# A spike-coded two-layer FFN: first layer over gathered w1 rows in two groups instead of over all 512 channels

## The chip, the core and the metric

The kernel runs on one core of one Trainium2 chip. The metric is the device time of one execution in microseconds; the kernel before takes 104.52 us in the median of 3 runs (104.49 to 104.67). The profile was taken in a further execution of 103.89 us, whose instructions span 102.1 us. Engines: PE (matrix unit; its weight load is PEld), DVE (vector), ACT (scalar), POOL (GpSimd), and SP, which only issues transfers. Two batches (b = 0, 1) of 2048 tokens with 512 channels; all data is float32.

## What is computed

```python
rates  = relu(x) * 0.001
c      = cond[:, None, :] + cumsum(rates, axis=1)      # per batch and channel
spikes = (floor(c) - floor(c one token before)) / 0.001
h      = relu(spikes @ w1 + b1)                        # 512 -> 2048
out    = x + h @ w2 + b2                               # 2048 -> 512
```

A channel climbs by less than one over a batch in nearly all cases, so it spikes at most once (with these inputs never more). Most of the 4096 tokens have no spike: their row is x plus one fixed row (the "idle row", relu(b1) @ w2 + b2). Counted from the reference's inputs: 421 and 427 channels spike in the two batches, on 386 and 380 different tokens; 33 and 40 of these tokens have more than one spiking channel, with 35 and 47 channels beside the first one of their token.

## The kernel before

The work has four parts, and their order on each engine is written out by hand.

**Table.** For a token with exactly one spiking channel the FFN's result depends on the channel alone. A table of 512 such rows (less the idle row) is computed for every channel: ACT turns each of the 16 chunks of transposed w1 into `relu(1000 * w1 + b1) - relu(b1)` (`table_chunk`, L419), and PE multiplies them with w2 into four PSUM banks (`table_part`, L799): 64 matmuls of 512 columns.

**Where the spikes are.** DVE sums relu(x) over each block of 16 tokens (`block_totals`), PE makes running sums (`sum_totals`), DVE finds the block in which each channel crosses its level (`find_blocks`), POOL fetches the 16 values of that block for each channel from a transposed copy of x (4 indirect transfers per batch, L342), and DVE finds the token (`find_bases`, `find_tokens`). PE copies the tokens along a row (`spread_tokens`), and DVE compares each channel's token with all others' (`count_met`): a channel alone on its token is a "single", the first one of several is a "lead" (`find_leads`). Leads get a slot number (`count_leads`, `find_slots`).

**Crowded tokens.** PE finds the token of every slot (PE's `find_slots`), DVE builds a 0/1 matrix of 512 channels by 128 slots (`first_spikes`, `second_spikes`), and `first_layer` (L883) multiplies w1 with it: 16 chunks of 4 matmuls, with 2 PSUM banks in turn, each emptied by ACT (L452). `second_layer` (L892) is 16 matmuls of 512 columns. DVE adds x and b2 (L729), and POOL writes the rows to their places (L381).

**All other rows.** The idle row is `idle_by_hand` on DVE for the first 9 chunks (`BY_HAND`), and `add_strips` and `join_strips` on PE for the rest. `add_idle` adds it to all of x in SBUF: DVE by four token rows at a time (L673), POOL by one (L354), in quarters (b, q). SP stores the eight quarters of 1 MB each in the fixed order (0,0), (0,3), (0,1), (0,2), (1,3), (1,0), (1,1), (1,2) (L303), each after a wait for its adds. Then POOL adds the table rows onto the rows of singles with indirect accumulating transfers, 4 per batch (L347). Those of batch b wait for `idle_stored[b]`, that is until all four stores of that batch have landed, and the first also for `singles_listed` and for `table_rows_ready`, ACT's copies of the table out of PSUM (L458), which stand between the first layer's evictions. The last write of new rows is behind them in POOL's order. POOL may touch x rows only between marks (`reading_psum`) that DVE sets.

The program ends when the last scatters and the write at L381 have landed. SP's queue also loads w1 (4 MB in 4 transfers, L297) behind all other loads.

## Time and profile before

| | |
|---|---|
| median of 3 runs | 104.52 us (104.49 to 104.67) |
| the profiled execution | 103.89 us, span 102.1 us |
| PE busy | 95.4 us (93%) |
| DVE busy | 65.9 us (64%) |
| POOL busy | 43.2 us (42%) |
| ACT busy | 35.5 us (35%) |
| moved by DMA | 31.66 MB, mean 310 GB/s |
| granted TensorE clock | 0.99 of full speed |

The span is cut into stages: table and search for spikes until about 68 us, first layer until 83 us, second layer until 97 us, and a tail of 4.7 us. Beside the two layers, SP stores the eight quarters (from 56 to 87 us) and POOL issues the scatters (from 77 to 95 us). Busy shares are averages over these stages; what one stage is worth shows in the waits and in the chain of work that ended last.

### The profile page before, as it was taken

How to read it: one execution, taken by the hardware profiler on the slowest of the kernel's cores; microseconds unless marked ns; L12 is line 12 of the kernel's file. 1: busy time of each engine (PE TensorE's matmuls, PEld its weight loads, DVE VectorE, ACT ScalarE, POOL GpSimd, SP SyncE). 2: the span in 40 equal slices, each digit the busy share in tenths (PEclk: the TensorE clock that was granted, in tenths of full speed). 3: DMA queues.
4: the chain of work that ended last, by engine and by line, in shares of the span. 5: the costliest groups of instructions: out<-in, count | busy, mean ns of one | idle time of the engine just before them, and what ended most of it. 6: DMA issues, size and time to landing. Idle time of an engine off the chain costs nothing.

```text
span 102.1 us, 1157 instructions
## 1 busy us (share of the span) xinstructions
PE 95.4 (93%) x370; PEld 54.0 (53%) x370; DVE 65.9 (64%) x142; ACT 35.5 (35%) x64; POOL 43.2 (42%) x44
## 2 busy tenths in 40 slices
PE   5999999999999999999969999999999999999910
PEld 5944444444644444644234564649999984444300
DVE  2448999888699999488958888899993020020020
ACT  2796515315372540569740000003953330000000
POOL 6350000000078700017508181499937883688040
PEclk9999999999999999999999999999999999999996
DMA  1999999999999999999999725427999999998701
GB/s 58 286 387 414 417 420 411 411 407 409 409 409 409 396 393 401 409 394 387 379 373 352 324 116 218 193 125 292 395 430 436 407 336 195 218 115 106 92 8 62
DMA packets 10028, 31.66 MB, mean 310 GB/s; under 512 B 1671, under 2 KB 1799, under 8 KB 8994
## 3 DMA queue, kind: packets, MB, share of 16 engines
q1 hardware_dynamic: 8304, 29.63, 74.7%
q0 software_dynamic: 1568, 1.90, 11.4%
q8 instruction: 5, 0.08, 0.3%
q14 instruction: 5, 0.04, 0.1%
q10 hardware_dynamic: 146, 0.01, 0.1%
HBM read 21.58 MB, written 10.75 MB: 316 GB/s over the span
## 4 chain that ended last, share of the span: by engine, by line
PE 50%; DVE 20%; POOL 13%; issue 11%; ACT 1%; POOLq 1%; DVEq 0%
PE ps_table L807 40%; DVE x_sb L673 11%; POOL out L347 11%; PE ps_small L900 4%; DVE same L600 3%; PE ps_idle L823 2%; PE ps_turn L844 2%; DVE hot L619 1%; PE ps_idle L827 1%; PE ps_idle L833 1%; DVE spk_t L634 1%; POOL out L381 1%; POOL general_x L370 1%; POOLq L258 1%; DVE spk_t L629 1%
## 5 line engine op out<-in xcount | busy, mean ns | idle before, releaser
L807 PE MATMUL ps_table<-w_sb 128*128 128x512 f32 x128 | 56.9, 595 | 0.0
L807 PEld LDWEIGHTS ps_table<-w_sb 128*128 128x128 f32 x128 | 23.6, 190 | 27.1 <-issue 26.4
L342 POOL DMA_INDIRECT rates<-in_x_turned,sixteen_at x8 | 9.9, 1236 | 33.9 <-DVE sixteen_at L563 32.1
L354 POOL TENSOR_TENSOR x_sb<-x_sb,idle_row 128x512 f32<-128x512 f32 x12 | 14.9, 1277 | 9.9 <-DVEq L706 3.7
L422 ACT ACTIVATE w_sb<-w_sb,b_col 128x512 f32<-128x512 f32 (+2 forms) x19 | 12.2, 643 | 16.5 <-DMA w_sb<-in_w_pairs 16.3
L549 DVE SCALAR_TENSOR_TENSOR total_two<-x_sb,total_two 128x1024 f32<-128x1024 f32 x14 | 17.1, 1225 | 1.2 <-DMA x_sb<-in_x 0.8
L347 POOL DMA_INDIRECT out<-w_sb,to_single x8 | 12.5, 1558 | 5.8 <-issue 3.7
L895 PE MATMUL ps_table<-w_sb 128*128 128x512 f32 x32 | 14.0, 595 | 0.0
L423 ACT ACTIVATE w_sb<-w_sb,minus_relu_b 128x512 f32<-128x512 f32 (+2 forms) x19 | 12.3, 649 | 0.6
L673 DVE TENSOR_TENSOR x_sb<-x_sb,ps_idle 128x2048 f32<-128x2048 f32 x5 | 11.2, 2283 | 1.5 <-ACT idle_row L448 1.3
L895 PEld LDWEIGHTS ps_table<-w_sb 128*128 128x128 f32 x32 | 6.0, 190 | 7.2 <-issue 6.9
L452 ACT ACTIVATE w_sb<-ps_turn,b_col 128x128 f32<-128x128 f32 x8 | 2.9, 367 | 19.0 <-PE ps_turn L888 18.4
L888 PE MATMUL ps_small<-spk_t,w_sb 128*128 128x128 f32 x64 | 8.5, 275 | 0.0
L888 PE MATMUL ps_turn<-spk_t,w_sb 128*128 128x128 f32 x64 | 8.5, 275 | 0.0
L888 PEld LDWEIGHTS ps_turn<-spk_t,w_sb 128*128 128x128 f32 x64 | 7.9, 192 | 0.5 <-DVE spk_t L634 0.3
L888 PEld LDWEIGHTS ps_small<-spk_t,w_sb 128*128 128x128 f32 x64 | 7.8, 192 | 0.0
L509 DVE SCALAR_TENSOR_TENSOR idle_part<-w_sb,relu_b,idle_part 128x512 f32<-128x512 f32 x9 | 6.7, 750 | 1.5 <-DMA w_sb<-in_w_pairs 1.4
L729 DVE TENSOR_TENSOR w_sb<-ps_table,general_x 128x512 f32<-128x512 f32 x1 | 0.7, 692 | 6.3 <-PE ps_table L895 6.3
L900 PE MATMUL ps_small<-ones 128*128 128x128 f32 x16 | 3.7, 427 | 1.1 <-POOLq L320 1.1
L727 DVE TENSOR_TENSOR general_x<-general_x,b_row 128x512 f32<-128x512 f32 x1 | 0.7, 691 | 6.2 <-DMA general_x<-in_x,from_general 6.2
L900 PEld LDWEIGHTS ps_small<-ones 128*128 128x128 f32 x16 | 3.5, 330 | 1.1 <-POOLq L320 1.1
L665 DVE TENSOR_SCALAR crowd<-ps_table 128x1 f32<-128x1 f32 x1 | 0.2, 159 | 6.1 <-PE ps_table L871 6.1
(113 smaller groups left out, 65.5 us busy)
## 6 DMA issues: line engine op xcount, KB each, us to landing
x_sb<-in_x SPq DMA_DIRECT2D x16, 512.0 KB, 14.3
out<-x_sb SPq DMA_DIRECT2D x8, 1024.0 KB, 4.1
w_sb<-in_w_pairs SPq DMA_DIRECT2D x15, 512.0 KB, 15.7
w_sb<-in_w SPq DMA_DIRECT2D x4, 1024.0 KB, 15.3
w_sb<-in_w_pairs SPq DMA_DIRECT2D x2, 256.0 KB, 2.9
b_row<-in_b SPq DMA_DIRECT2D x1, 256.0 KB, 15.3
rates<-in_x_turned,sixteen_at POOLq DMA_INDIRECT x8, 6.5
out<-w_sb,to_single POOLq DMA_INDIRECT x8
```

The source lines that it names most:

```text
L342: pool.indirect_dma_start(out=rates[:, col, :], out_offset=None, in_=x_sixteen, in_offset=bass.IndirectOffsetOnAxis(ap=sixteen_at[:, col:c ...
L347: pool.indirect_dma_start(out=out_rows, out_offset=bass.IndirectOffsetOnAxis(ap=to, axis=0), in_=row, in_offset=None, bounds_check=last_ro ...
L354: last = pool.tensor_tensor(x_sb[b][:, t, :], x_sb[b][:, t, :], idle_row[:, :], ALU.add)
L422: chain(act.activation(weights, weights, ACT.Relu, bias=b1_col[:, m:m + 1], scale=PER_DT))
L423: act.activation(weights, weights, ACT.Identity, bias=minus_relu_b1[:, m:m + 1]).then_inc(table_hidden_ready, 1)
L509: step = dve.scalar_tensor_tensor(out=idle_part[:, :], in0=w2_sb[:, m, :], scalar=relu_b1[:, m:m + 1], in1=idle_part[:, :], op0=ALU.mult, ...
L549: chain(dve.scalar_tensor_tensor(out=total_two[b][:, :, :], in0=tokens, scalar=0.0, in1=total_two[b][:, :, :], op0=ALU.max, op1=ALU.add))
L673: last = dve.tensor_tensor(tokens, tokens, along(ps_idle[:, :], end - begin), ALU.add)
L807: last = pe.matmul(ps_table[c][:, :], table_hidden[:, m, c * P:(c + 1) * P], w2_sb[:, m, :], start=(m == 0), stop=(m == FC - 1))
L888: last = pe.matmul(ps_hidden[m % 2][:, 0:P], w1_sb[:, c, m * P:(m + 1) * P], spk_t[:, c, :], start=(c == 0), stop=(c == DC - 1))
L895: last = pe.matmul(ps_out[:, :], hidden[m], w2_sb[:, m, :], start=(m == 0), stop=(m == FC - 1))
L900: pe.matmul(ps_small[:, 0:P], ones[:, :], ones[:, :], start=True, stop=True)
```

## The change

First layer: POOL gathers rows of w1 (8 KB each), one for every channel that shares its token with others, into two SBUF arrays that are cleared at the start. Group 0 holds the lead channel of every crowded token, at the token's slot; group 1 holds all other channels on crowded tokens, in slots of their own. Each chunk of the first layer is then two matmuls: group 0's rows times the identity, and group 1's rows times `others_turn`, a 0/1 matrix that says to which slot's token each of the others belongs. There are three PSUM banks in turn in place of two. The 4 MB load of w1 goes away (it remains in the repeat path that these inputs don't take). To list the rows, DVE makes one-hot matrices for both groups, PE multiplies them with a small array `named` (block, token in block, row of 128, partition), and DVE turns the result into row numbers.

Around it: five chunks of the idle row by hand in place of nine, so 12 strips on PE in place of 8; another order of DVE's and PE's steps; ACT copies the table out of PSUM only after all evictions of the first layer; DVE adds the idle row to 24 token rows and POOL to 8, in place of 20 and 12.

```diff
-    BY_HAND = 9
+    BY_HAND = 5
+    GROUPS = 2
@@ SP
-            for i in range(WQ):
-                part = slice(i * (F // WQ), (i + 1) * (F // WQ))
-                sp.dma_start(w1_sb[:, :, part], w1.rearrange("(c p) f -> p c f", p=P)[:, :, part]).then_inc(w1_in[i], 16)
@@ POOL
+            for g in range(GROUPS):
+                pool.memset(spiking_rows[g][:, :], 0.0).then_inc(rows_cleared, 1)
...
+            def get_rows(b):
+                pool.wait_ge(rows_cleared, GROUPS)
+                for g in range(GROUPS):
+                    n = b * GROUPS + g
+                    pool.wait_ge(rows_listed, n + 1)
+                    if b > 0:
+                        pool.wait_ge(rows_got[g], 16 * b)
+                    pool.indirect_dma_start(out=spiking_rows[g][:, :], out_offset=None, in_=w1,
+                                            in_offset=bass.IndirectOffsetOnAxis(ap=row_at[:, n:n + 1], axis=0),
+                                            bounds_check=last_channel, oob_is_err=False).then_inc(rows_got[g], 16)
+
+            get_rows(0)
             pool.wait_ge(idle_copied, 1)
             pool.wait_ge(reading_psum, 1)
-            add_idle(0, 12, 14)
+            add_idle(0, 12, 13)
+            get_rows(1)
             pool.wait_ge(reading_psum, 2)
-            add_idle(0, 14, 16)
-            pool.wait_ge(reading_psum, 3)
+            add_idle(0, 13, 16)
             add_idle(1, 12, 16)
-            add_idle(1, 8, 12)
             pool.wait_ge(singles_listed, 1)
@@ ACT
             for m in range(FC):
                 relu_hidden(m, hidden_summed, m + 1, hidden_ready)
-                if 1 <= m <= DC:
-                    act.activation(table_row[m - 1], ps_table[m - 1][:, :], ACT.Copy).then_inc(table_rows_ready, 1)
+            for c in range(DC):
+                act.activation(table_row[c], ps_table[c][:, :], ACT.Copy).then_inc(table_rows_ready, 1)
@@ DVE, new steps
+            def list_rows(b):
+                for g in range(GROUPS):
+                    n = b * GROUPS + g
+                    dve.wait_ge(lists_found, n + 1)
+                    chain(dve.tensor_scalar(row_of[:, b, g, :], ps_list[g][:, b, 2:3], float(P), NO_ROW, ALU.mult, ALU.add))
+                    dve.tensor_tensor(row_at[:, n:n + 1], row_of[:, b, g, :], ps_list[g][:, b, 3:4], ALU.add).then_inc(
+                        rows_listed, 1)
...
+            def turn_others():
+                dve.wait_ge(row_tokens_spread, 1)
+                chain(dve.tensor_scalar(others_turn[:, :], ps_tokens, row_token[:, 1, :], None, ALU.is_equal))
+                dve.sem_inc(others_ready, 1)
@@ PE
+            def first_layer():
+                pe.wait_ge(rows_got[0], 16 * B)
+                pe.wait_ge(rows_got[1], 16 * B)
+                pe.wait_ge(others_ready, 1)
                 for m in range(FC):
-                    if m >= 2:
-                        pe.wait_ge(ready, base + m - 1)
-                    for c in range(DC):
-                        last = pe.matmul(ps_hidden[m % 2][:, 0:P], w1_sb[:, c, m * P:(m + 1) * P],
-                                         spk_t[:, c, :], start=(c == 0), stop=(c == DC - 1))
-                    yield last
+                    if m >= HB:
+                        pe.wait_ge(hidden_ready, m - HB + 1)
+                    chunk = slice(m * P, (m + 1) * P)
+                    pe.matmul(ps_hidden[m % HB][:, 0:P], spiking_rows[0][:, chunk], ident[:, :], start=True, stop=False)
+                    pe.matmul(ps_hidden[m % HB][:, 0:P], spiking_rows[1][:, chunk], others_turn[:, :],
+                              start=False, stop=True).then_inc(hidden_summed, 1)
```

**DVE, the end of the pass over x.** In the rows, `total_two<-x_sb` is one eighth of a batch in `block_totals`, `rates` to `token` is `find_tokens`, and `same,met` is `count_met`. Before, from `find_bases(0)` on:

```order
L575 SCALAR_TENSOR_TENSOR token_base<-blocks_under,far 128x4
L549 SCALAR_TENSOR_TENSOR total_two<-x_sb,total_two 128x1024
L509 SCALAR_TENSOR_TENSOR idle_part<-w_sb,relu_b,idle_part 128x512
L549 SCALAR_TENSOR_TENSOR total_two<-x_sb,total_two 128x1024 x2
L552 TENSOR_TENSOR total<-total_two 128x512
L559 TENSOR_TENSOR under<-ps_turn,theta_sum 128x512
L562 TENSOR_REDUCE blocks_under<-under 128x4
L563 SCALAR_TENSOR_TENSOR sixteen_at<-blocks_under,sixteen_f 128x4
L582 TENSOR_SCALAR rates<-rates 128x64
```

The same place in the changed kernel:

```order
L617 SCALAR_TENSOR_TENSOR token_base<-blocks_under,far 128x4
L590 SCALAR_TENSOR_TENSOR total_two<-x_sb,total_two 128x1024 x2
L624 TENSOR_SCALAR rates<-rates 128x64
L625 SCALAR_TENSOR_TENSOR climb<-token_keep,rates 128x64
L627 TENSOR_TENSOR climb<-climb,sum_at 128x64
L628 TENSOR_TENSOR under<-climb,theta 128x64
L629 TENSOR_REDUCE tokens_under<-under 128x4
L630 TENSOR_SCALAR named<-tokens_under 128x4
L631 SCALAR_TENSOR_TENSOR token<-tokens_under,token_base 128x4
L590 SCALAR_TENSOR_TENSOR total_two<-x_sb,total_two 128x1024 x2
L593 TENSOR_TENSOR total<-total_two 128x512
L644 SCALAR_TENSOR_TENSOR same,met<-ps_met,token,weigh 128x512
```

`find_tokens(0)`, which waits for POOL's four gathers of batch 0, now stands ahead of the last quarter of batch 1's sums.

**POOL, from the gathers of `rates` to the scatters.** `x_sb<-x_sb,idle_row` is one token row of `add_idle`. Before:

```order
L342 DMA rates<-in_x_turned,sixteen_at 128x16 x3
L354 TENSOR_TENSOR x_sb<-x_sb,idle_row 128x512 [waits reading_psum,idle_copied]
L354 TENSOR_TENSOR x_sb<-x_sb,idle_row 128x512
L354 TENSOR_TENSOR x_sb<-x_sb,idle_row 128x512 [waits reading_psum]
L354 TENSOR_TENSOR x_sb<-x_sb,idle_row 128x512
L354 TENSOR_TENSOR x_sb<-x_sb,idle_row 128x512 [waits reading_psum]
L354 TENSOR_TENSOR x_sb<-x_sb,idle_row 128x512 x7
L347 DMA out<-w_sb,to_single 4096x512 [waits table_rows_ready,idle_stored0,singles_listed]
```

Now:

```order
L362 DMA rates<-in_x_turned,sixteen_at 128x16 x3
L386 DMA spiking_rows<-in_w,row_at 128x2048 [waits rows_listed,rows_cleared]
L386 DMA spiking_rows<-in_w,row_at 128x2048 [waits rows_listed]
L374 TENSOR_TENSOR x_sb<-x_sb,idle_row 128x512 [waits reading_psum,idle_copied]
L386 DMA spiking_rows<-in_w,row_at 128x2048 [waits rows_got0,rows_listed,rows_cleared]
L386 DMA spiking_rows<-in_w,row_at 128x2048 [waits rows_got1,rows_listed]
L374 TENSOR_TENSOR x_sb<-x_sb,idle_row 128x512 [waits reading_psum]
L374 TENSOR_TENSOR x_sb<-x_sb,idle_row 128x512 x6
L367 DMA out<-w_sb,to_single 4096x512 [waits table_rows_ready,idle_stored0,singles_listed]
```

One token row of quarter (0,3) is added ahead of the gathers of w1's rows for batch 1, the other three behind them and behind DVE's second mark.

## Rows read from the trace of the kernel before

**Rows 1.** The page: the chain that ended last, by engine.

```profile
PE 50%; DVE 20%; POOL 13%; issue 11%; ACT 1%; POOLq 1%; DVEq 0%
```

**Rows 2.** Groups by line: count, busy us, mean ns, idle before.

```profile
L888 PE MATMUL ps_small<-spk_t,w_sb 128*128 128x128 f32 x64 | 8.5, 275 | 0.0
...
L452 ACT ACTIVATE w_sb<-ps_turn,b_col 128x128 f32<-128x128 f32 x8 | 2.9, 367 | 19.0 <-PE ps_turn L888 18.4 <-issue 0.5
```

**Rows 3.** Timeline, PE, both layers: start, duration, what.

```profile
68.93 1.05 PE L888 MATMUL ps_turn<-spk_t,w_sb 128*128 128x128 f32 x8
...
83.36 13.98 PE L895 MATMUL ps_table<-w_sb 128*128 128x512 f32 x32
```

**Rows 4.** Timeline, DVE, end of the pass over x.

```profile
36.62 1.23 DVE L549 SCALAR_TENSOR_TENSOR total_two<-x_sb,total_two 128x1024 f32<-128x1024 f32 x1
...
40.00 1.23 DVE L549 SCALAR_TENSOR_TENSOR total_two<-x_sb,total_two 128x1024 f32<-128x1024 f32 x1 [0.24 <-DMA x_sb<-in_x]
41.26 0.69 DVE L552 TENSOR_TENSOR total<-total_two 128x512 f32<-128x512 f32 x1
43.59 0.69 DVE L559 TENSOR_TENSOR under<-ps_turn,theta_sum 128x512 f32<-128x512 f32 x1 [1.63 <-PE ps_turn L844]
```

**Rows 5.** Timeline, POOL, gathers of rates.

```profile
34.53 0.96 POOL L342 DMA_INDIRECT rates<-in_x_turned,sixteen_at  x1 [0.30 <-issue]
45.58 0.94 POOL L342 DMA_INDIRECT rates<-in_x_turned,sixteen_at  x1 [10.09 <-DVE sixteen_at L563]
```

**Rows 6.** Line L342, issues at 32.5 and 34.5: issue to landing.

```profile
DMA to landing us min/median/max: 5.3/5.8/6.3
```

**Rows 7.** Groups by line, DVE and POOL.

```profile
L600 DVE SCALAR_TENSOR_TENSOR same<-ps_turn,token,weigh 128x512 bf16<-128x512 f32 x4 | 3.0, 751 | 0.4 <-PE ps_turn L856 0.3
L354 POOL TENSOR_TENSOR x_sb<-x_sb,idle_row 128x512 f32<-128x512 f32 x12 | 14.9, 1277 | 9.9 <-DVEq L706 3.7 <-DVEq L714 3.4 <-DVEq L597 2.7
L673 DVE TENSOR_TENSOR x_sb<-x_sb,ps_idle 128x2048 f32<-128x2048 f32 x5 | 11.2, 2283 | 1.5 <-ACT idle_row L448 1.3 <-DVE hot L619 0.2
```

**Rows 8.** Timeline, DVE, from find_tokens(1) on.

```profile
56.10 0.42 DVE L582 TENSOR_SCALAR rates<-rates 128x64 f32<-128x64 f32 x1
...
65.15 2.29 DVE L673 TENSOR_TENSOR x_sb<-x_sb,ps_idle 128x2048 f32<-128x2048 f32 x1 [0.24 <-DVE hot L619]
...
68.39 6.67 DVE L673 TENSOR_TENSOR x_sb<-x_sb,ps_idle 128x2048 f32<-128x2048 f32 x3
```

**Rows 9.** Line L301: the first store's landing; the fourth store's issue.

```profile
DMA to landing us min/median/max: 4.1/4.1/4.1
...
L301 SPq DMA_DIRECT2D out<-x_sb x1: 332/332/332, 70.7 to 70.7; - x1
```

**Rows 10.** Stages, busy us per engine, then clock, DMA share, GB/s.

```profile
76.00:80.00 4.00, 4.00 (x39) 4.00 (x38) 1.27 (x11) 1.63 (x5) 2.72 (x2) 1.00 0.99 410
```

**Rows 11.** DMA of 86 to 87 us: packets, MB, share of 16 engines.

```profile
q0 software_dynamic: 142, 0.19, 109.8%
q1 hardware_dynamic: 2, 0.01, 2.2%
```

**Rows 12.** Timeline, POOL, the tail.

```profile
76.98 1.61 POOL L347 DMA_INDIRECT out<-w_sb,to_single  x1 [1.92 <-issue]
...
84.45 1.01 POOL L370 DMA_INDIRECT general_x<-in_x,from_general  x1 [0.30 <-issue]
87.52 1.56 POOL L347 DMA_INDIRECT out<-w_sb,to_single  x1 [2.06 <-DMA out<-x_sb]
...
93.09 1.55 POOL L347 DMA_INDIRECT out<-w_sb,to_single  x1 [0.30 <-issue]
98.42 1.03 POOL L381 DMA_INDIRECT out<-w_sb,to_general  x1 [3.79 <-DVE w_sb L729]
```

**Rows 13.** Timeline, DVE, the new rows; line L381, issue to landing.

```profile
97.45 0.69 DVE L729 TENSOR_TENSOR w_sb<-ps_table,general_x 128x512 f32<-128x512 f32 x1 [6.32 <-PE ps_table L895]
...
DMA to landing us min/median/max: 2.7/2.7/2.7
```

More of the change, by code:

```diff
@@ L612, in find_leads @@
                 dve.sem_inc(leads_ready, 1)
             def find_slots(b):
-                mine = own(b)
                 dve.wait_ge(leads_before, b + 1)
-                chain(dve.scalar_tensor_tensor(out=slot[:, mine], in0=leads_run[:, mine], scalar=ps_small[:, b:b + 1],
-                                               in1=leads[:, mine], op0=ALU.add, op1=ALU.mult))
-                chain(dve.tensor_tensor(hot[:, mine, :], over(slot[:, mine], P), along(slot_name[:, :], DC), ALU.is_equal))
-                dve.sem_inc(hot_ready, 1)
+                for g in range(GROUPS):
+                    dve.scalar_tensor_tensor(out=slot[:, b, g, :], in0=leads_run[:, b, g, :],
+                                             scalar=ps_count[:, b, g:g + 1], in1=leads[:, b, g, :],
+                                             op0=ALU.add, op1=ALU.mult).then_inc(dve_step, 1)
@@ new lines, in find_slots @@
+                steps[0] += GROUPS
+                dve.wait_ge(dve_step, steps[0])
+                for g in range(GROUPS):
+                    dve.tensor_tensor(hot[:, b, g, :, :], over(slot[:, b, g, :], P), along(slot_name[:, :], DC),
+                                      ALU.is_equal).then_inc(hot_ready, 1)
+            def list_rows(b):
+                for g in range(GROUPS):
+                    n = b * GROUPS + g
[3 more added lines that the diff above has]
+                        rows_listed, 1)
@@ new lines, in find_row_tokens @@
+            def find_row_tokens():
+                for g in range(GROUPS):
+                    dve.tensor_copy(token_parts[:, g, :], ps_list[g][:, 0, 0:2]).then_inc(dve_step, 1)
+                steps[0] += GROUPS
+                dve.wait_ge(dve_step, steps[0])
+                for g in range(GROUPS):
+                    dve.tensor_tensor(token_parts[:, g, :], token_parts[:, g, :], ps_list[g][:, 1, 0:2],
+                                      ALU.add).then_inc(dve_step, 1)
+                steps[0] += GROUPS
+                dve.wait_ge(dve_step, steps[0])
+                chain(dve.scalar_tensor_tensor(out=row_token[:, :, :], in0=token_parts[:, :, 0:1], scalar=float(BLK),
+                                               in1=token_parts[:, :, 1:2], op0=ALU.mult, op1=ALU.add))
+                dve.sem_inc(row_tokens_ready, 1)
@@ L870, in sum_checks @@
                 pe.wait_ge(table_rows_ready, DC)
-                pe.matmul(ps_checks[:, 0:2], ones[:, :], checks[:, :], start=True, stop=True).then_inc(checks_summed, 1)
-            def find_slots(b):
-                pe.wait_ge(hot_ready, b + 1)
-                if b == 0:
-                    pe.wait_ge(met_counted, 1)
-                for c in range(DC):
-                    col = b * DC + c
-                    last = pe.matmul(ps_slots[:, b * P:(b + 1) * P], token[:, col:col + 1].to_broadcast([P, P]),
-                                     hot[:, col, :], start=(c == 0), stop=(c == DC - 1))
-                last.then_inc(slots_found, 1)
@@ L883, in first_layer, with list_rows @@
-            def first_layer(ready, base):
-                for m in range(FC):
-                    if m >= 2:
-                        pe.wait_ge(ready, base + m - 1)
+                pe.matmul(ps_checks, ones[:, :], checks[:, :], start=True, stop=True).then_inc(checks_summed, 1)
+            def list_rows(b):
+                for g in range(GROUPS):
+                    pe.wait_ge(hot_ready, b * GROUPS + g + 1)
+                    for c in range(DC):
+                        last = pe.matmul(ps_list[g][:, b, :], hot[:, b, g, c, :], named[:, b, c, :],
+                                         start=(c == 0), stop=(c == DC - 1))
+                    last.then_inc(lists_found, 1)
@@ L892, in second_layer @@
-            def second_layer(ready, base):
+                    last.then_inc(again_hidden_summed, 1)
+            def second_layer(to, ready, base):
                 for m in range(FC):
-                    pe.wait_ge(ready, base + m + 1)
-                    last = pe.matmul(ps_out[:, :], hidden[m], w2_sb[:, m, :], start=(m == 0), stop=(m == FC - 1))
+                    if m == FC // 2 and to is ps_out:
+                        sum_checks()
+                    pe.wait_ge(ready, base + (max(m + 1, OUT_FREE) if to is ps_out else m + 1))
+                    last = pe.matmul(to[:, :], hidden[m], w2_sb[:, m, :], start=(m == 0), stop=(m == FC - 1))
```

226 lines of the change are left out of this document (122 added, 104 removed).

## Prediction

> **What bounds the kernel now.** I read the chain of work that ended last, then the groups by line, then the timelines of PE, DVE and POOL, then the transfers. The chain gives PE half of the span, DVE a fifth, POOL an eighth [rows 1]. PE runs almost without a gap: the table, then from 68.93 us the first layer, and from 83.36 the second [rows 3]. DVE adds the new rows at 97.45, POOL writes them from 98.42 [rows 12, 13], and the span ends at 102.1, 3.7 us after that. So PE's two layers set the end.
>
> But a second chain ends almost as late, on DVE, the store queue and POOL: DVE's last add of the idle row ends at 75.06 (68.39 + 6.67) [rows 8]; the first scatter starts at 76.98; those of batch 1 wait for batch 1's stores until 87.52; the last one ends at 94.64 [rows 12]. It has 98.42 - 94.64 = 3.8 us of slack. That slack is what the change must not use up.
>
> **PE's part.** The first layer takes 83.2 - 68.9 = 14.3 us for 64 float32 matmuls, 0.223 each (the group rows count two passes per matmul, in two banks of 64 passes each) [rows 2, 3]. It becomes 32: 7.15 us, a gain of 7.15. ACT's evictions don't hold it: 0.37 us per chunk [rows 2] in a chunk of 0.45, and a third bank gives two chunks of time for the way round.
>
> The first layer starts later, though. PE loses eight slot matmuls (1.8 us) and gains four strips (0.9), 16 bf16 matmuls of four columns (about 1.2, an estimate between 0.5 and 1.8, since no such form is in the trace) and a transpose (0.3). It also waits in its own order for DVE, as worked out next. I find its table finished near 72.5.
>
> **DVE's part.** `find_tokens(0)` moves ahead of the last quarter of batch 1's sums. It needs POOL's fourth gather of batch 0, issued at 34.53 [rows 5] and landed 5.3 us later [rows 6], at 39.8. DVE would be there at about 37: so far `find_bases(0)` is done at 36.6 [rows 4]; the change takes one eighth of x (1.23) and two hand chunks (0.75 each) from ahead of it, and puts two eighths behind it: 36.6 - 2.7 + 2.5 = 36.4, and up to 37.5 where DVE waits for x. The gathers may be issued up to a microsecond earlier with less DVE work beside them. I take 39.2. Queued behind this wait are find_tokens (1.55 us), two eighths of x (2 x 1.26) and `total` (0.7): batch 1's total is ready at 44.0, against 41.95 [rows 4], 2.0 us late; between 0.8 (gathers a microsecond faster) and 2.7. The removed hand chunks (4 x 0.75 = 3.0 us) so buy nothing: they only lengthen the wait. PE's `sum_totals(1)` and all behind it in PE's order wait for the same.
>
> From there: 1.65 us to `under` (43.59 - 41.95, [rows 4]), 2.0 more to POOL's first gather of batch 1 (45.58 - 43.59) [rows 4, 5], three steps of 1.25 to the fourth (51.3), and 2.7 to 5.3 us to landing. The queue is empty by then, since w1 is no longer loaded; I take 3.5: 54.8. DVE's own work up to there (three compares of 0.75 [rows 7], leads, bases, slots with two one-hot writes of about 0.7, and a short wait for PE's count) comes to 54.9, so neither waits long.
>
> Then `find_tokens(1)` to the mark behind which the large adds run. Before, this took 65.15 - 56.10 = 9.05 us [rows 8]. Now: tokens 1.6; wait for PE's lists and two row lists 1.4; wait for the spread and four compares 3.8; leads 0.8; half an add 1.2; slots and two one-hots with the wait for PE 2.2; half an add 1.2; two row lists 0.85; row tokens 0.8; odd checks 1.0; `turn_others` 0.4: 15.2 us. Mark 2 comes at 70.1. Behind it DVE has five adds of 2.28 [rows 7], until 81.6, then the singles' list, 82.2.
>
> POOL in the meantime gathers w1's rows for batch 1 from 67.9 to 70.2, and only then, behind mark 2, adds the last three token rows of quarter (0,3): 3 x 1.28 [rows 7], until 73.9. The store of (0,3) is second in SP's fixed order. So only one quarter is stored before 74.2, and seven go out behind it. Before, two were gone by 66 us, and the fourth was issued at 70.7 [rows 9].
>
> **The stores.** The queue moves about 0.405 MB per us when it is full [rows 10]: 7 x 1.049 MB take 18.1 us, to 92.3. Landing adds 1.7 (4.1 for a store of 2.4 us of data) [rows 9]. The scatters of batch 0 and the fetch of x rows run beside the end. Before, five stores issued from 70.7 had landed at 87.5, 16.8 us, against 12.9 + 1.7: they lost about 2 us. I take 1.7 and get 95.7; bounds are 94.0 (nothing lost) and 99 (all of the scatters' data first).
>
> The Trainium skill ("DMA: Bandwidth & Descriptors", Queues, rings and completion order) says that each DMA engine takes turns between its queues, packet by packet. By that rule alone the scatters' five or so microseconds of engine time (an estimate) would nearly all be added to the stores, and the sum would be 3 us higher. The trace does not bear that out fully: only from 86 us, when the stores' queue is down to 2.2%, does the software queue fill the engines [rows 11].
>
> **The end.** Batch 1's scatters take 94.64 - 87.52 = 7.1 us [rows 12]: 95.7 to 102.8. POOL then loads the repeat count, which before lay in its wait: 0.3 to 1.1 us, I take 0.5. The write starts at 103.3 and the span ends 3.7 later [rows 12, 13], at 107.0, against 102.1: 4.9 us longer. The profiled execution's own time was 103.89, so 108.8; the median of the runs is 0.63 higher, so 109.4.
>
> PE's chain is done well before: its two layers end 21.4 us after the first matmul (97.45 - 68.93 - 7.15). From 73.2 that is 94.6. Its gain is covered by POOL's wait, and even a first layer that stayed at 14.3 us would end the span at about 106.5.
>
> **Rivals.**
> *PE's chain still sets the end (faster).* The place is POOL's wait for batch 1's stores. Were they landed by about 87.5, and the first scatter out by 77, POOL would be done by 94.6 and the end would be 94.6 + 4.7 = 99.3: 2.8 us less, 101.7 in the median. It decides as soon as batch 1's stores land by 87 and the table copies and the list of singles are there by 78. For it speaks PE's share of the chain [rows 1], and 4 MB less to load. Against it: the table copies now follow all evictions (73.2 + 7.15 + about 1.2 = 81.6), and seven stores from 74 can't be done by 87 at 0.405 MB per us. How late PE starts hangs on the last gather of w1's rows, issued at 69.2. The nearest rows have a landing at 2.7 us [rows 13] and one at 6.3 [rows 6]: 72 to 75.5.
> The Trainium skill (same page, "Anatomy of one DMA — SWDGE (gpsimd) path") gives about 2.0 us plus bytes over 436 GB/s; for 47 rows of 8 KB that is an estimate of 2.9 us. No row here has a gather of that size.
>
> *POOL's own work sets the end, not the stores (slower by less).* First scatter at 82.9 (singles' list 82.2), then as before 7.5 to the fetch of x, 1.3, 7.1 for batch 1 [rows 12]: 98.8, write at 99.3, span 103.0: 105.4 in the median. It needs stores landed by 91.7, so the mark and POOL's adds some 4 us earlier than I find.
>
> *DVE doesn't stall at the gather, and everything on DVE is 2 us earlier.* Same mechanism, stores land near 93.7: 107.4. It lies in the forecast's own range.
>
> *The change doesn't do what it says:* a channel list over 128 slots would start the repeat path, far slower. With 73 leads and 82 others it doesn't.
>
> **Numbers.** Forecast (stores late, scatters behind them): 0.67, its own range 106.3 to 111.5, from the bounds 94.0 and 99 of the stores and 0.8 to 2.7 of the stall. POOL's own work: 0.15. PE's chain: 0.11. Ends that cancel to about nothing: 0.03. Above 111.5: 0.04. A difference under 0.2% can't be told from none; from the same cases: faster 0.12, same 0.03, slower 0.85. Range 103.8 to 111.5: it takes in POOL's own work and leaves out the fast case.
>
> **What would show it.** Right: a wait of DVE for the gathers between the fifth and seventh eighth of batch 1, 1 us or more; `total(1)` near 44; DVE's last add near 81.6; the second store issued near 74; POOL idle before the first scatter of batch 1 with a store as what ended it, near 95.7; the first layer at 7 to 7.5 us; the chain of waits running through stores and scatters. Wrong: the write of new rows released by DVE as before; stores landed by 90; or a fill of the queue by w1's row gathers that holds PE past 78.

## The result, and the profile after

| | before | after |
|---|---|---|
| median of 4 runs on one chip | 104.5 us (103.96 to 104.67) | 109.34 us (108.88 to 109.98) |
| the profiled execution, its span | 103.89, 102.1 us | 109.98, 108.1 us |
| granted TensorE clock, mean | 0.99 | 0.94 |

The changed kernel takes 1.048 times as long (95% interval 1.041 to 1.054). The forecast was 109.4 us. Part of that closeness is luck: the forecast span was 107.0, and the spans of the four runs are 107.1 to 108.1, the profiled one being the longest; I had added 0.63 us from the profiled time to the median, and this time the median lies 0.64 below. So the mechanism is to be judged by the rows, not by the last digit.

The chain of work that ended last, by engine (answers to [rows 1]):

```profile
PE 46%; POOL 14%; DVE 13%; DMA 11%; issue 8%; POOLq 3%; ACT 1%; DVEq 0%
```

PE still has the largest share, because the chain runs back through the table. Its end is what changed. POOL's timeline (start, duration, what, in brackets the idle time before it and what ended it), which answers to [rows 12]:

```profile
68.10 0.99 POOL L386 DMA_INDIRECT spiking_rows<-in_w,row_at  x1 [5.64 <-DVE row_at L679]
69.40 1.00 POOL L386 DMA_INDIRECT spiking_rows<-in_w,row_at  x1 [0.30 <-issue]
70.43 8.65 POOL L374 TENSOR_TENSOR x_sb<-x_sb,idle_row 128x512 f32<-128x512 f32 x7
87.60 1.60 POOL L367 DMA_INDIRECT out<-w_sb,to_single  x1 [8.52 <-ACT w_sb L493]
...
95.05 1.01 POOL L402 DMA_INDIRECT general_x<-in_x,from_general  x1 [0.30 <-issue]
96.37 1.56 POOL L367 DMA_INDIRECT out<-w_sb,to_single  x1 [0.30 <-issue]
...
101.94 1.54 POOL L367 DMA_INDIRECT out<-w_sb,to_single  x1 [0.30 <-issue]
103.78 1.03 POOL L413 DMA_INDIRECT out<-w_sb,to_general  x1 [0.31 <-issue]
```

The write of new rows starts at 103.8 in place of 98.4, and follows at once on POOL's own scatters. From the first scatter on POOL works without a gap for 103.78 - 87.60 = 16.2 us. Batch 1's scatters, which I had waiting for a store, wait for nothing. The one wait is ahead of the first scatter, 8.5 us, for ACT's copies of the table (L493). The chain of waits has that place in the order of time (start, duration, engine and tile):

```profile
85.61 0.24 PE ps_turn L956 x2
85.85 0.02 issue
85.87 0.37 ACT w_sb L487
86.24 0.98 ACT w_sb L493 x2
87.22 0.37 issue
87.60 1.60 POOL out L367
```

The last chunk of the first layer, its eviction, the copies, the scatter: PE is back on the path that sets the end, though not through its second layer.

The new rows themselves are ready long before the write. DVE's timeline, as [rows 13]:

```profile
99.23 0.69 DVE L788 TENSOR_TENSOR general_x<-general_x,b_row 128x512 f32<-128x512 f32 x1 [5.45 <-DMA general_x<-in_x,from_general]
99.96 0.69 DVE L790 TENSOR_TENSOR w_sb<-ps_met,general_x 128x512 f32<-128x512 f32 x1
```

They are there at 100.65 (99.96 + 0.69), 3.1 us ahead of the write: PE's gain is covered, as forecast. PE's timeline at the first layer, answering to [rows 3], and the stages there (PE, PEld, DVE, ACT, POOL busy with counts, granted clock, DMA share, GB/s):

```profile
75.77 0.76 PE L955 MATMUL ps_turn<-ident,spiking_rows 128*128 128x128 f32 x2 [3.72 <-issue]
76.33 0.63 PE L956 MATMUL ps_turn<-others_turn,spiking_rows 128*128 128x128 f32 x2
...
82.10 0.39 PE L955 MATMUL ps_small<-ident,spiking_rows 128*128 128x128 f32 x2
```

```profile
68.00:72.00 4.00, 3.79 (x10) 1.50 (x9) 3.34 (x8) 0.00 (x0) 3.56 (x4) 1.00 0.88 297
72.00:76.00 4.00, 0.28 (x2) 0.26 (x2) 4.00 (x3) 0.00 (x0) 4.00 (x4) 0.82 0.62 248
76.00:80.00 4.00, 4.00 (x20) 4.00 (x21) 4.00 (x3) 1.47 (x4) 3.08 (x3) 0.50 1.00 412
80.00:84.00 4.00, 4.00 (x32) 4.00 (x31) 1.69 (x7) 2.56 (x7) 0.00 (x0) 0.82 1.03 426
```

PE is idle from 72.0 to 75.8, until the rows of w1 are there. Behind that wait the granted clock is 0.50, the lower of the two levels (1.2 GHz), until about 81 us: a float32 matmul (two passes in the trace, the `x2` of the rows) starts every 0.43 us there, and every 0.22 us later. The first layer takes 9.9 us (75.77 to 85.67) where I had 7.15.

### The profile page after: what moved, and what is told of

The parts are those of the page before. It is cut to its first block, busy times and chain, and to the rows that moved or that the text cites. A ratio compares the mean times of both kernels' runs of the same rounds, so it can differ in the third digit from the quotient of the medians.

```text
span 108.1 us, 1064 instructions
## 1 busy us (share of the span) xinstructions
PE 92.8 (86%) x315; PEld 48.1 (44%) x315; DVE 69.3 (64%) x163; ACT 35.4 (33%) x64; POOL 44.3 (41%) x46
## 4 chain that ended last, share of the span: by engine, by line
PE 46%; POOL 14%; DVE 13%; DMA 11%; issue 8%; POOLq 3%; ACT 1%; DVEq 0%
PE ps_table L868 27%; POOL out L367 9%; DMA rates<-in_x_turned,sixteen_at 6%; DMA spiking_rows<-in_w,row_at 5%; PE ps_small L978 3%; POOL rates L362 3%; DVE same L644 3%; DVE total_two L590 2%; DVE x_sb L736 2%; POOLq L59 2%; PE ps_turn L955 2%; PE ps_turn L905 2%; PE ps_idle L884 2%; PE ps_turn L956 2%; PE ps_small L956 1%
## 5 line engine op out<-in xcount | busy, mean ns | idle before, releaser
L868 PE MATMUL ps_table<-w_sb 128*128 128x512 f32 x128 | 58.5, 603 | 0.0
L868 PEld LDWEIGHTS ps_table<-w_sb 128*128 128x128 f32 x128 | 23.8, 193 | 27.1 <-issue 25.3
L973 PE MATMUL ps_met<-w_sb 128*128 128x512 f32 x32 | 14.1, 595 | 0.0
L736 DVE TENSOR_TENSOR x_sb<-x_sb,ps_idle 128x2048 f32<-128x2048 f32 (+1 forms) x7 | 13.5, 1979 | 0.4 <-DVE others_turn L699 0.2
L374 POOL TENSOR_TENSOR x_sb<-x_sb,idle_row 128x512 f32<-128x512 f32 x8 | 9.9, 1267 | 0.0
L973 PEld LDWEIGHTS ps_met<-w_sb 128*128 128x128 f32 x32 | 5.9, 190 | 6.7 <-issue 6.7
L386 POOL DMA_INDIRECT spiking_rows<-in_w,row_at x4 | 4.0, 1002 | 11.8 <-DVE row_at L679 11.2
L955 PE MATMUL ps_turn<-ident,spiking_rows 128*128 128x128 f32 x12 | 3.1, 354 | 3.7 <-issue 3.7
L546 DVE SCALAR_TENSOR_TENSOR idle_part<-w_sb,relu_b,idle_part 128x512 f32<-128x512 f32 x5 | 3.9, 778 | 1.6 <-DMA w_sb<-in_w_pairs 1.5
L955 PEld LDWEIGHTS ps_turn<-ident,spiking_rows 128*128 128x128 f32 x12 | 2.5, 259 | 4.5 <-issue 4.5
```

The source lines that it names most:

```text
L374: last = pool.tensor_tensor(x_sb[b][:, t, :], x_sb[b][:, t, :], idle_row[:, :], ALU.add)
L736: last = dve.tensor_tensor(tokens, tokens, along(ps_idle[:, :], end - begin), ALU.add)
L868: last = pe.matmul(ps_table[c][:, :], table_hidden[:, m, c * P:(c + 1) * P], w2_sb[:, m, :], start=(m == 0), stop=(m == FC - 1))
L955: pe.matmul(ps_hidden[m % HB][:, 0:P], spiking_rows[0][:, chunk], ident[:, :], start=True, stop=False)
L973: last = pe.matmul(to[:, :], hidden[m], w2_sb[:, m, :], start=(m == 0), stop=(m == FC - 1))
```

## The experiments

Each kernel is the changed one with the edit shown, unless said otherwise. Ratios are to the kernel before, run in turn with it on the same chip: 103.11 us for the first four, 104.18 for the next four, 104.29 for the last four. Compare ratios, best within one of these groups; the changed kernel's own are 1.048, and 1.043 when run again. A span, and every time read from a timeline, is that of one profiled execution (108.1 and 107.8 for the changed kernel); the runs of one kernel differ by about 1 us, and the profiled one can be the fastest or the slowest of them. Times of the changed kernel are from its first profile unless said otherwise.

### One wait at a time: the table copies, the clock, the second gather

**Copies early** (`e1`):

```diff
                 relu_hidden(m, hidden_summed, m + 1, hidden_ready)
-            for c in range(DC):
-                act.activation(table_row[c], ps_table[c][:, :], ACT.Copy).then_inc(table_rows_ready, 1)
+                if 1 <= m <= DC:
+                    act.activation(table_row[m - 1], ps_table[m - 1][:, :], ACT.Copy).then_inc(table_rows_ready, 1)
```

> The changed kernel, with ACT's four copies of the table out of PSUM back between the first layer's evictions of chunks 1 to 4, as in the kernel before. If the late copies hold the first scatter (87.60 in the changed kernel's trace), it now comes at 81.6 to 82.5, released by DVE's list of singles or the stores of batch 0. What ends the kernel then tells the next limit. Stores next (the prediction's mechanism): batch 1's scatters wait for a store until about 94.5, the write of new rows is at about 102, the time is about 2 us less, 107.4. PE next: no wait for stores, the write follows DVE's new rows at 100.7, 3 us less, 106.2. If the copies don't hold anything: 109.3 again.

Measured: ratio 1.063 (1.055 to 1.072), span 107.6. **PE busy** (`e2`) fills PE's wait:

```diff
             table_part(15, 1, DC)
+            for _ in range(16):
+                pe.matmul(ps_turn[:, 0:P], ones[:, :], ones[:, :], start=True, stop=True)
             first_layer()
```

> The changed kernel, with 16 matmuls of 128x128 on constants (3.6 us at full clock) between the table and the first layer, where PE now waits 3.7 us for the gathered rows; their results are overwritten. If the halved granted clock of 76 to 81 us comes from that wait, the clock stays at 1.0 there, the first layer takes 7.15 us in place of 9.9, the first scatter comes 2.7 us earlier (84.9), and the time falls by 2.0 to 2.7, to 106.6 to 107.3 (the lower saving if batch 1's stores, landed at about 94, take over). If the clock falls for another reason: 9.9 us again and 109.3. If the added matmuls delay the first layer: slower.

Measured: 1.060 (1.048 to 1.072), span 108.4. **Both** (`e3`):

> Both edits: early copies of the table and PE kept busy while it waits. First scatter at 81.6 to 82.5, DVE's new rows at about 97.9. If batch 1's stores are the next limit, batch 1's scatters start at about 94.5 as in the kernel with early copies alone, so this one is no faster than that one: 107.3. If PE is: the write at 98.2 to 99, and the time 5 us less than the changed kernel's, 104.3, even with the kernel before.

Measured: 1.065 (1.057 to 1.072), span 107.2. The changed kernel wasn't in that group of runs, so a difference of a per cent from its 1.048 can't be read out of these ratios; but they exclude that the end came forward by the 2.1, 2.8 and 4.7 us by which the first scatter did (85.54, 84.84 and 82.92). Of the 4.7 us in `e3`, 1.1 are no effect of the edits: its profiled execution is the fastest of its five, and DVE's large adds start at 68.84 there against 69.91. Where the rest went is in POOL's timeline of `e3`:

```profile
82.92 1.60 POOL L367 DMA_INDIRECT out<-w_sb,to_single  x1 [4.87 <-issue]
...
95.26 1.56 POOL L367 DMA_INDIRECT out<-w_sb,to_single  x1 [3.87 <-DMA out<-x_sb]
...
102.68 1.03 POOL L413 DMA_INDIRECT out<-w_sb,to_general  x1 [0.31 <-issue]
```

The first scatter is 4.7 us earlier, and batch 1's only 1.1, which is the 1.1 of the earlier start and nothing more, because now a store holds them. `e1` and `e2` show the same, at 95.53 and 95.90. The last store in `e3` was issued at 81.0 and took 14.0 us to land (the line of the stores, issue to landing):

```profile
DMA to landing us min/median/max: 3.9/6.9/14.0
```

So batch 1's stores land at 95.0 here (81.0 + 14.0). In the changed kernel they land sooner, though they were issued later: by 94 in its first profile, whose store queue shows no packet after that, and at 94.9 in its second (the last one issued at 82.4, 12.5 us to landing). POOL's own work is ready for batch 1 at 96.37 and 96.07, at least 2.4 us later in the one and 1.2 in the other. So an earlier first scatter goes with later stores. The rows give a reason, though no run tests it alone: the scatters' packets then run beside the last stores, and from 89 to 93 us `e3` moves 1.12 MB of stores, 0.28 MB per us (queue: packets, MB, share of 16 engines; q1 are the stores, q0 is POOL's queue):

```profile
q1 hardware_dynamic: 153, 1.12, 81.7%
q0 software_dynamic: 133, 0.17, 24.8%
```

From 86 to 87 us, with no scatter's packet beside them, the stores moved 0.43 MB in one microsecond.

The copies were at 76.0 to 78.8 in `e3` and the list of singles at 80.4, so the first scatter at 82.9 waited for a third thing, batch 0's stores, which landed at 82.1; the profile names these in `e4` and `e10`. It is the same in `e1` (landed 84.7, scatter 85.54), so its expected 81.6 to 82.5 was missed.

In `e2` the clock stays at 1.00 and the first layer takes 7.2 us (75.69 to 82.91):

```profile
76.00:80.00 4.00, 4.00 (x38) 4.00 (x37) 4.00 (x3) 2.95 (x9) 2.96 (x3) 1.00 1.01 416
```

That settles the size: the term of 7.15 us was right at the full clock, and the wait in front of it cost 2.7 us of it.

**No second gather of w1 rows** (`e4`):

```diff
-            get_rows(1)
...
-                pe.wait_ge(rows_got[0], 16 * B)
-                pe.wait_ge(rows_got[1], 16 * B)
+                pe.wait_ge(rows_got[0], 16)
+                pe.wait_ge(rows_got[1], 16)
```

> The changed kernel without the gather of w1 rows for batch 1's crowded tokens (their part of the result is left out). PE has no gather to wait for at 72. If the landing of these rows holds the first layer: it starts at 72.0, the clock stays at 1.0, it ends near 79.2, copies are done by 82, and the first scatter comes at about 81.6, 6 us earlier. POOL also has 2.3 us more for its adds, so the stores start at about 72.5 and batch 1's have landed by about 92. Time 105 to 106. If the landing doesn't matter (PE waits for DVE or the lists): the first layer still starts at 75 or later and the time stays within 1 us of 109.3.

Measured: 1.046 (1.035 to 1.057), 108.4 us and not 105 to 106, span 106.3. The first layer starts at 71.6 and keeps the clock (to 78.7). POOL's timeline:

```profile
69.58 8.69 POOL L374 TENSOR_TENSOR x_sb<-x_sb,idle_row 128x512 f32<-128x512 f32 x7 [7.44 <-DVEq L776]
83.09 1.60 POOL L367 DMA_INDIRECT out<-w_sb,to_single  x1 [4.82 <-DMA out<-x_sb]
...
94.66 1.56 POOL L367 DMA_INDIRECT out<-w_sb,to_single  x1 [3.10 <-DMA out<-x_sb]
```

PE's start moved by 4.2 us and the copies with it, and batch 1's scatters by only 1.7, with POOL's adds starting 0.85 us sooner and two transfers fewer ahead of the stores. Both waits are for stores. (This kernel leaves out part of the result.)

### The stall at the gather, and the order on DVE

The changed kernel once more, beside the next three:

> The changed kernel unedited, on the chip of the kernels that follow, to have its ratio to the kernel before there: 1.04 to 1.06.

Measured: 1.043 (1.033 to 1.053), span 107.8; the same waits as the first time.

**DVE doesn't wait for the gathers** (`e6`; PE's order follows DVE's):

```diff
-            block_totals(1, 4, 6)
-            find_tokens(0)
-            block_totals(1, 6, XH)
-            count_met(0, 0, 1)
-            find_blocks(1)
-            count_met(0, 1, DC)
+            block_totals(1, 4, XH)
+            find_tokens(0)
+            find_blocks(1)
+            count_met(0, 0, DC)
...
-            spread_tokens(0)
             table_part(10, 0, 1)
             sum_totals(1)
-            table_part(10, 1, DC)
+            table_part(10, 1, 2)
+            spread_tokens(0)
+            table_part(10, 2, DC)
```

> The changed kernel with find_tokens(0) behind all eighths of x on DVE, and PE's sum_totals(1) ahead of spread_tokens(0). This undoes the move that the prediction blames for 2 us. If it is right: no wait of DVE for the gathers, total(1) at 42 in place of 45.3, DVE's mark 2 and the stores about 2.5 us earlier, the first layer about 2.5 us earlier, the time 2 to 3 us less than the changed kernel's: ratio to before about 1.025. If the stall is made good later (DVE waits for PE or the gathers of batch 1 anyway), mark 2 stays at 69 to 70 and the time within 0.7 us.

Measured: 107.63 us, against 109.26 for the changed kernel in the same group: 1.030 (1.022 to 1.039), span 106.1. The intervals touch, but DVE's timelines leave no doubt on the place. The changed kernel, then `e6`, where DVE waits 1.76 us for x itself instead:

```profile
40.36 0.20 DVE L624 TENSOR_SCALAR rates<-rates 128x64 f32<-128x64 f32 x1 [2.99 <-DMA rates<-in_x_turned,sixteen_at]
...
42.07 2.48 DVE L590 SCALAR_TENSOR_TENSOR total_two<-x_sb,total_two 128x1024 f32<-128x1024 f32 x2
44.59 0.69 DVE L593 TENSOR_TENSOR total<-total_two 128x512 f32<-128x512 f32 x1
```

```profile
41.81 0.69 DVE L593 TENSOR_TENSOR total<-total_two 128x512 f32<-128x512 f32 x1
42.42 0.19 DVE L624 TENSOR_SCALAR rates<-rates 128x64 f32<-128x64 f32 x1
```

Batch 1's `total` is ready at 42.5 and not at 45.3. The gathers of w1's rows for batch 1 come at 65.87 and not at 68.00 (both here are of the changed kernel's second profile), batch 1's scatters at 93.59 and not at 96.07.

**Three adds of POOL ahead of its gathers** (`e5`: `e3` and this):

```diff
-            add_idle(0, 12, 13)
+            add_idle(0, 12, 16)
             get_rows(1)
             pool.wait_ge(reading_psum, 2)
-            add_idle(0, 13, 16)
```

> Early copies and PE kept busy, as before, and POOL adds all four token rows of quarter (0,3) in its wait of 62.5 to 67.9 us for the second row list, in place of one there and three behind the gathers. If the stores of batch 1 are what holds the end of the version with early copies and busy PE (its batch 1 scatters started at 95.3, released by a store), two stores are gone by 72, the burst starts at 72 with six quarters, batch 1's stores have landed at 89 to 91, and the write of new rows comes at about 99: 3.5 us earlier, time 103.5 to 105, level with the kernel before. If something else holds the end there, the write stays at 102 to 103.

Measured: 1.088 (1.078 to 1.098), span 111.9: clearly worse than everything else. DVE's timeline, beside POOL's four adds from 60.86 to 65.77:

```profile
61.55 4.25 DVE L650 SCALAR_TENSOR_TENSOR is_first<-met,valid 128x4 f32<-128x4 f32 x1
65.84 0.16 DVE L652 TENSOR_TENSOR leads<-valid,is_first 128x4 f32<-128x4 f32 x1
```

An operation on four elements a partition, 0.16 us in itself, takes 4.25 us and ends with POOL's last add. The gathers for batch 1 came at 71.75, against 67.03 in `e3`. A second loss of about 4 us came on top: these gathers are now behind the two stores of 70.4 and 70.8 and beside those that follow, and take 8.9 and 10.0 us to land, against at most 6.2 in `e3`. (All four gathers of `e5`, issue to landing:)

```profile
DMA to landing us min/median/max: 4.5/7.1/10.0
```

PE starts the first layer at 83.17, 8.6 us later than in `e3`. No run separates the two losses; the store of (0,3), which the edit was to bring forward, likely has its part in the second.

**All of these** (`e8`: `e5` and `e6`, with the lists of singles ahead of DVE's last three adds, and half an add behind `find_row_tokens`):

```diff
+            list_singles()
+            list_general()
             add_idle(1, 0, 4)
             add_idle(1, 4, 8)
             add_idle(1, 8, 12)
-            list_singles()
-            list_general()
...
-            add_idle(0, 2, 4)
             list_rows(1)
             find_row_tokens()
+            add_idle(0, 2, 4)
```

> All of these together (early copies, PE busy, quarter (0,3) early, no stall), with the list of singles ahead of batch 1's adds and half an add moved behind the row lists. Estimated: gather of rows issued at 65 to 66, landed at 72, first layer 73 to 80.2, DVE's new rows at 95, batch 1's stores landed at 87 to 88, last scatter at 95, write at 95.5 to 96, span about 100: 2 us less than the kernel before, ratio 0.98. If the stores or POOL's scatters still hold the end: 1.00 to 1.01.

Measured: 1.067 (1.056 to 1.077), span 110.4. The same 4.25 us stand at 59.44, and the last gather takes 9.4 us to land; what the other edits give doesn't make up for it.

### The stores: their order, and their number

**Orders only** (`e9`: `e1`, `e6`, 14 fillers on PE, the lists ahead as in `e8`, and SP's order by readiness):

```diff
-for b, q in ((0, 0), (0, 3), (0, 1), (0, 2), (1, 3), (1, 0), (1, 1), (1, 2)):
+for b, q in ((0, 0), (0, 1), (0, 3), (0, 2), (1, 0), (1, 1), (1, 3), (1, 2)):
```

> No stall of DVE, early copies, PE kept busy (14 matmuls), the list of singles ahead of batch 1's adds, and SP's stores in the order in which the quarters become ready: (0,0), (0,1), (0,3), (0,2), (1,0), (1,1), (1,3), (1,2). POOL's adds stay between the marks. Burst of seven stores from 70.0 in place of 72.2, batch 1's landed near 91.5, write of new rows at 99, span 102.7: ratio to the kernel before 1.00 to 1.01. If POOL's own chain still holds the end: first scatter at 80, end 101 to 102, ratio 0.99 to 1.00. If neither moves: 1.03.

Measured: 1.031 (1.024 to 1.037), span 106.6. I had expected 1.00 to 1.01. The first scatter leaves at 81.0, 6.6 us earlier than in the changed kernel, and against `e6` (1.030) it buys nothing: batch 1's wait 5.06 us for a store, until 94.56. The stores gained little because scatters' packets run beside them from 85 us on, and because the lists, now ahead, ran beside POOL's adds (68.08 to 76.73), and DVE's last add ended at 84.1, in spite of a start 2 us sooner. DVE's timeline:

```profile
69.76 2.28 DVE L736 TENSOR_TENSOR x_sb<-x_sb,ps_idle 128x2048 f32<-128x2048 f32 x1
71.96 4.80 DVE L703 TENSOR_TENSOR single<-is_first,leads 128x8 f32<-128x8 f32 x1
...
77.41 6.67 DVE L736 TENSOR_TENSOR x_sb<-x_sb,ps_idle 128x2048 f32<-128x2048 f32 x3
```

**Two stores fewer** (`e10`: `e3`, with SP's list cut behind (1,0) and the waits for batch 1 at two stores):

> The version with early copies and busy PE, less the last two stores (quarters (1,1) and (1,2) of x plus the idle row are not written; batch 1's scatters wait for two stores). If stores hold its end: the scatters of batch 1 follow the fetch of x rows at once, at 91.7 in place of 95.3, the last one ends at 98.8, the write follows DVE's new rows (98.5 to 99.2 there) at 99.5, span 103.3, 3.9 us less: ratio 1.02 in place of 1.06. If something else in the queue holds them (the software queue's own backlog): they start at 95 again and the ratio stays at 1.05 to 1.06.

Measured: 1.017 (1.010 to 1.024), span 104.5. POOL's timeline:

```profile
83.22 1.60 POOL L367 DMA_INDIRECT out<-w_sb,to_single  x1 [5.14 <-DMA out<-x_sb]
...
92.00 1.56 POOL L367 DMA_INDIRECT out<-w_sb,to_single  x1 [0.30 <-issue]
...
99.41 1.03 POOL L413 DMA_INDIRECT out<-w_sb,to_general  x1 [0.30 <-issue]
```

This is the test that the store theory needed. `e3` and `e10` start their scatters within 0.3 us of each other; with two stores gone (the kernel leaves out those rows) batch 1's go 3.3 us earlier and the write comes 3.3 us earlier (102.68 to 99.41). The ratio is 1.017 in place of 1.065, but across two groups of runs; the 3.3 us are the better measure.

**Two orders** (`e11`: the edit of `e6` and SP's order of `e9`, and nothing else):

> The kernel without DVE's stall, with SP's stores in the order of readiness, and nothing else (copies late, PE waits idle). Its parent measured 1.030; POOL's scatters of batch 1 started at 93.6, held by a store. With the burst 2 us earlier stores land at 91.5, but the first scatter still waits for ACT's late copies (83.6), so POOL's chain would start batch 1 at 92.4: 1.2 us less, ratio 1.02.

Measured: 1.020 (1.013 to 1.026), span 104.5, the best full kernel of the changed kind and still slower than the one before. Against `e6` (1.030, another group) the gain isn't clear of noise in the ratios; the timelines show it, 1.0 us for batch 1's scatters. Its copies are late as in the changed kernel (POOL's timeline):

```profile
83.81 1.60 POOL L367 DMA_INDIRECT out<-w_sb,to_single  x1 [7.01 <-ACT w_sb L493]
...
92.58 1.56 POOL L367 DMA_INDIRECT out<-w_sb,to_single  x1 [0.30 <-issue]
```

Batch 1's scatters no longer wait for a store (in `e6` they did, 1.52 us).

### The kernel before with late copies

**`e7`**, the only one built on the kernel before: ACT's copies moved behind all evictions, the edit of `e1` backwards.

> The kernel before, with ACT's four copies of the table behind all evictions of the first layer, as in the changed kernel. The first scatter moves from 77.0 to 84.2. Batch 1's scatters then start at 93.4, behind POOL's own chain, and the last ends at 100.6; PE also waits about 2.4 us ahead of the second layer (its check sums need the copies), so DVE's new rows come at 99.9. Both give a write at 100.8 to 101 in place of 98.4: 2.4 us more, ratio 1.023. If the place of the copies is free: 1.00.

Measured: 1.041 (1.034 to 1.049), span 106.8, nearly twice what I expected. The first scatter is at 85.04 (8.1 later than in [rows 12]), and PE, which needs those banks too, stood still in front of the second layer. PE's timeline:

```profile
85.77 0.35 PE L871 MATMUL ps_table<-checks,ones 128*128 128x2 f32 x2 [2.50 <-ACT w_sb L458]
85.98 15.68 PE L895 MATMUL ps_table<-w_sb 128*128 128x512 f32 x32
```

The second layer takes 15.68 us against 13.98 [rows 3], with a granted clock of 0.82 and 0.76 in the two stages from 84 us on. So this edit alone costs about as much as the whole change, but by PE's way: there the write waits for the new rows (DVE, 101.78). It doesn't show that the copies are what the changed kernel loses by; `e1` shows that they are not, taken alone.

## Why the prediction was right, point by point

The direction and the time came out. Of the mechanism, the part up to the start of the stores held; the part behind it, which fixes the end, held only in part.

- **A stall of DVE in front of batch 1's sums.** Right: 2.99 us, `total` ready 45.3 against my 44.0. I had it 1.3 us early. The fourth gather was issued at 34.04, 0.5 us sooner than before, within the gain that I had allowed; but the wait behind it ended 6.3 us after its issue, and I had taken 5.3. The stall's price, 2.0 in the sum, is 1.6 us by `e6` in the medians and 1.7 in the spans (an edit that also reorders PE).
- **Mark 2, the last add, the second store.** 69.9, 81.0 and 74.2, against 70.1, 81.6 and 74.2. Right, in spite of the point above, because the steps between took 24.6 us (45.3 to 69.9) and not 26.1.
- **First layer 7.15 us from 73.2.** This step failed most. PE finished the table at 72.0, as I had it within 0.5, but the last gather, issued at 69.40, landed about 6.3 us later, near my upper bound (75.5) and not where I put it. The landings of the four gathers, issue to landing:

```profile
DMA to landing us min/median/max: 4.5/5.5/6.3
```

  The Trainium skill's estimate of 2.9 us (the page and section that the prediction named) is less than half of that; the measurement decides. And behind the 3.7 us wait came the halved clock, which I hadn't considered at all: 2.7 us (`e2`).
- **First scatter at 82.9.** It was 87.6. My copies were done at 81.6, ahead of the list of singles; the ones that mattered came at 87.2, and the 5.6 us are 2.6 of a later start, 2.7 of clock and 0.3 of the rest. The list was there at 81.5, as forecast within a microsecond. `e3`, with the copies early and the clock kept, has it at 82.9, though by another condition: batch 0's stores. I had left these out. By my own figures their last one lands at 83.7 (74.2 + 3 x 2.59 + 1.7), and in the changed kernel it did at 83.1, so the scatter could not start before about 84 even with early copies.
- **Stores of batch 1 landed at 95.7, and the write behind them.** The main term of the sum, and it failed for the changed kernel in size and role. The stores landed by 94 and at 94.9 in its two profiles; the scatters' 1.7 us in their way was hardly lost there, since the scatters' packets began when the stores' data was nearly through (in the first profile it ended at 93, where my sum without it had 92.3). With earlier scatters, in `e1`, `e2` and `e3`, it is lost: batch 1's scatters, held by a store, start at 95.3 to 95.9. What set the end of the changed kernel is the rival "POOL's own work": batch 1's scatters at 96.37 and 96.07, the write at 103.8 and not at 99.3, because POOL's start was 4.7 us later than I had it. The forecast named the wrong one of two mechanisms and gave it 0.67 against 0.15; the time came out because the other one, late by the landing of the gathers and by the clock, ended within a microsecond of the same place. That is luck.
- **The range.** Its upper end doesn't follow from its bounds: stores at 99 in place of 95.7 alone give 112.7, and the range stopped at 111.5.
- **The load of the repeat count, 0.5 us.** It cost nothing that can be seen: the write follows at 0.31, POOL's usual gap.
- **PE's gain covered.** Right: 3.1 us lie between the new rows and the write. `e2` makes PE's first layer 2.7 us shorter and `e4` starts it 4.2 us earlier; batch 1's scatters move by 0.5 and 1.7 us, to where a store releases them.
- **Faster by the PE chain.** It needed stores landed by 87 and a first scatter by 77. With all eight stores the earliest landing is that of `e11`, at 90, and the earliest first scatter is at 81.0 (`e9`).

Where does the loss lie, then? In that both chains behind DVE's large adds are full: seven stores that start at 74, and nine transfers that POOL issues in 16.2 us. One removed shows the other within about a microsecond (`e1`, `e2`, `e3`); it takes both (`e10`), or something ahead of both (`e6`, `e11`), to move the end. `e11` is at 2.0 per cent in place of 4.3 to 4.8, by order alone. What the rest is was not separated: mark 2 comes 4.8 us later than the same place before (69.9 against 65.15), of which the stall is about half, and neither the longer steps behind it nor the split of 24 and 8 token rows was undone; nor was `e11` run with early copies, a busy PE, and nothing with two SBUF inputs beside POOL's adds.

## What to carry to other kernels

Before an engine's work is shortened, look for how much slack the next chain has, and then what *that* chain starts on: here PE was to give 7 us; the chain over DVE, SP and POOL had 3.8 us in hand, and the change spent more than that on a wait, a later mark and late copies. When two waits end within a microsecond, an experiment that removes one doesn't tell its cost; remove both, or what lies ahead of both. Ask too whether the two share something: here an earlier scatter took from the stores what it had won. And a wait on PE costs more than its length, if the matmuls behind it then run at half the clock.

## What the runs showed of the hardware that I had not expected

**DVE blocked by a train of POOL's adds.** A DVE operation with both inputs in SBUF, started while POOL adds rows in SBUF, ended only with POOL's last add: 4.25 us in `e5` and `e8`, 4.80 in `e9`, for work of 0.16 us. Beside a single add, in the changed kernel, the same operation as in `e5` took 0.67 us and ended with that add (at 62.5). Operations with one input in PSUM, as DVE's adds of 2.28 us, ran beside the same adds in their usual time (2.28 us in `e9` at 69.76, and 2.283 on average in [rows 7]). The Trainium skill ("SBUF — State Buffer", "Reading the diagram" and "Who interferes with whom") says that such an operation and one of GpSimd that reads SBUF exclude each other for a whole instruction. The runs agree on who blocks whom, and show more: DVE didn't get its turn between POOL's three or four consecutive adds, but after the last. The changed kernel has at most one add of POOL beside such an operation; my edits of `e5`, `e8` and `e9` put a train of them there.

**Scatters that start late beside stores, and then slow them.** Transfers of the changed kernel from 91 to 92 us, from 92 to 93 and from 93 to 94 (q1 the stores, q0 POOL's queue, as above):

```profile
q1 hardware_dynamic: 48, 0.39, 107.9%
```

```profile
q1 hardware_dynamic: 36, 0.26, 89.7%
q0 software_dynamic: 9, 0.01, 5.3%
```

```profile
q0 software_dynamic: 140, 0.18, 108.9%
q1 hardware_dynamic: 12, 0.00, 0.7%
```

POOL issued its first scatter at 87.60 and the third at 91.37, yet q0 has no packet at all in any microsecond from 87 to 92. Taken alone this looks as if POOL's queue had to wait until the stores' queue runs out, as in [rows 11]. The other runs show two things. First a delay: with stores under way, the first packet comes 4 to 7 us after the first issue (issue at 82.92 and packet between 89 and 90 in `e3`, 81.02 and 85 to 86 in `e9`). In `e7`, where the stores' last data was through and the last one landed at 85.8, it is 2 to 3 us: issue at 85.04, and this row from 87 to 88 us:

```profile
q0 software_dynamic: 58, 0.08, 84.9%
```

What makes the delay wasn't tried. Then the two queues do share the engines, from 89 to 93 us in `e3` (the rows above) and from 85 to 93 in `e9`, with stores left to move all the while. The turns that the Trainium skill tells of ("DMA: Bandwidth & Descriptors", "Queues, rings and completion order") fit that stretch, in which both queues have packets in every microsecond; they don't tell of the delay ahead of it. In the changed kernel the delay reaches to the stores' last data, and so nothing was shared.
